# Sums of a chunk one step later, beside the other native products, and a new order of ScalarE's work in a graph layer

## The reference

```python
q = (x @ Wq).reshape(n, 8, 16)
wk = mlp2(edge_features, k_w1, k_b1, k_w2, k_b2)        # and wv: relu(e @ w1 + b1) @ w2 + b2
k = tensor_product(x[src], edge_sh, wk, Cqk)            # w * sum_{d,s} x[d] sh[s] C[d,s,:]; and v with wv, Cv
attn = einsum('ehd,ehd->eh', q[dst], k)
alpha = segment_softmax(attn, dst)
upd = segment_sum(v * alpha, dst) @ W_out
y = batchnorm(x @ W_self + upd) * gamma + beta
x1 = layernorm(x + y)
agg = segment_sum(e, dst) / max(count, 1)
out = layernorm(x1 + mlp3(concat([agg, x1])))
```

## Time and profile before

| | us |
|---|---|
| median of 3 runs (lowest, highest) | 5025.27 (5015.23, 5030.12) |
| the profiled execution's own time | 5049.76 |
| its span | 5047.8 |
| TensorE busy in the span | 4772.7 (95%) |
| VectorE, ScalarE, GpSimd busy | 4058.6, 3414.7, 3713.3 |

### The profile page before, as it was taken

One profiled execution on the slowest core, in us unless ns is written; L12 is line 12 of the kernel. 1 busy time (PEld: TensorE's weight loads), 2 busy tenths in 40 slices (PEclk: granted clock), 3 DMA queues, 4 the chain that ended last, 5 costly groups with the idle time before them and its releaser, 6 DMA issues. The chain is left out here.

```text
span 5047.8 us, 115383 instructions
## 1 busy us (share of the span) xinstructions
PE 4772.7 (95%) x35582; PEld 4503.5 (89%) x35582; DVE 4058.6 (80%) x5044; ACT 3414.7 (68%) x6495; POOL 3713.3 (74%) x3494
## 2 busy tenths in 40 slices
PE   7999999999999999999999999999999999998256
PEld 6999999999999999999999999999999999998143
DVE  5888888888888888888888888888888888886435
ACT  2677677677777767767777677777777777776137
POOL 3777777777777777777777777777777777774460
PEclk9999999999999999999999999999999999998578
DMA  8899999999999999999999999999999999996220
GB/s 218 202 215 210 208 210 214 208 214 210 212 207 214 213 208 213 211 210 211 211 213 211 207 216 213 216 214 214 213 216 212 214 214 216 212 213 158 91 68 26
DMA packets 693458, 1006.45 MB, mean 199 GB/s; under 512 B 120054, under 2 KB 378168, under 8 KB 693160
## 3 DMA queue, kind: packets, MB, share of 16 engines
q1 hardware_dynamic: 574856, 753.93, 65.7%
q0 software_dynamic: 112960, 242.16, 22.7%
q10 hardware_dynamic: 5600, 9.83, 0.7%
HBM read 826.64 MB, written 178.93 MB: 199 GB/s over the span
## 5 line engine op out<-in xcount | busy, mean ns | idle before, releaser
L825 PE MATMUL psum<-chi,zhi 128*128 128x256 f32 x7840 | 2316.9, 301 | 2.2 <-DVE rv L731 2.1
L535 POOL DMA_INDIRECT gq<-qtab,idxs x1568 | 1881.1, 1200 | 478.0 <-issue 475.8
L828 PE MATMUL psum<-clo,zhi 128*128 128x256 f32 x7840 | 2144.4, 282 | 0.0
L530 POOL DMA_INDIRECT gx<-in_xg,idxs x1568 | 1555.4, 992 | 465.0 <-issue 453.5
L827 PE MATMUL psum<-chi,zlo 128*128 128x256 f32 x6272 | 1768.4, 282 | 0.0
L825 PEld LDWEIGHTS psum<-chi,zhi 128*128 128x128 f32 x7840 | 1478.6, 189 | 99.3 <-issue 99.3
L828 PEld LDWEIGHTS psum<-clo,zhi 128*128 128x128 f32 x7840 | 1476.2, 188 | 0.0
L827 PEld LDWEIGHTS psum<-chi,zlo 128*128 128x128 f32 x6272 | 1183.6, 189 | 93.0 <-issue 93.0
L685 DVE TENSOR_TENSOR z<-psum,shb 128x1536 f32<-128x1536 f32 (+1 forms) x784 | 1130.5, 1483 | 126.2 <-PE psum L797 118.7
L580 ACT ACTIVATE zhi<-z 128x1536 fp32r<-128x1536 f32 (+1 forms) x784 | 993.5, 1267 | 247.9 <-DVE z L685 244.0
L710 DVE TENSOR_TENSOR zlo<-z,zhi 128x1536 fp32r<-128x1536 f32 (+1 forms) x784 | 922.2, 1217 | 0.0
(11 more groups left out here) (210 smaller groups left out, 6335.1 us busy)
## 6 DMA issues: line engine op xcount, KB each, us to landing
shb<-in_shT SPq DMA_DIRECT2D x392, 640.0 KB
shb<-in_shT SPq DMA_DIRECT2D x392, 512.0 KB
rows<-ot SPq DMA_DIRECT2D x392, 416.0 KB
e<-in_eT SPq DMA_DIRECT2D x392, 128.0 KB
drow<-rankd SPq DMA_DIRECT2D x392, 128.0 KB
gx<-in_xg,idxs POOLq DMA_INDIRECT x1568
gq<-qtab,idxs POOLq DMA_INDIRECT x1568
qtab<-qs ACTq DMA_DIRECT2D x25, 256.0 KB, 5.7
```

Source lines behind the costliest of these rows:

```text
L530: nc.gpsimd.indirect_dma_start(out=gx[:, s, k, :], out_offset=None, in_=xg[:, :], in_offset=bass.IndirectOffsetOnAxis(ap=ids[:, k:k + 1], ...
L535: nc.gpsimd.indirect_dma_start(out=gq[:, s, k, :], out_offset=None, in_=qtab[:, :], in_offset=bass.IndirectOffsetOnAxis(ap=ids[:, TC + k:T ...
L825: mm(tpb[:, k, :], zhi[:, s, j, e], chi[:, j, :], start=(j == 0), stop=False)
L828: last = mm(tpb[:, k, :], zhi[:, s, j, e], clo[:, j, :], start=False, stop=(j == ST - 1))
```

## The change

The sums of a chunk move to the next step (a = t - 7). On TensorE their first half goes to the head of the step and their second half behind `hidden(c)`, so that the native products stand together. On ScalarE the copies of the sums come first, `hid` and `hidhi` stand ahead of the second part of z, and `segments(b)` stands ahead of `feature_rows`. SyncE's store opens the step and is of chunk t - 8; `targets` is of chunk t - 5. The second mask tile `nmb` and its DMA go: the backward scan reads `nmf` shifted by one, with a last column set once to -1e30. The main stage has one more (mostly empty) step at its end.

```diff
@@ SyncE @@
-                        for ahead, tile in ((0, nmf), (1, nmb)):
-                            src = newd[bass.ds(g.value() * CH + ahead, GT * P)].rearrange("(t e) -> t e", t=GT)
-                            sp.dma_start(tile[:, s, :], src.unsqueeze(1).broadcast_to([GT, H, P])).then_inc(nm_in[s], 16)
+                        src = newd[bass.ds(g.value() * CH, GT * P)].rearrange("(t e) -> t e", t=GT)
+                        sp.dma_start(nmf[:, s, 0:P], src.unsqueeze(1).broadcast_to([GT, H, P])).then_inc(nm_in[s], 16)
...
                     def step(t, find, fetch, count):
+                        if (t + (-LAG - 2)).there():
+                            store(t + (-LAG - 2))
                         if (t + 2).there():
                             harmonics(t + 2)
                         if (t.r + 3) % 2 == 0 and (t + 3).there():
                             features(t + 3)
-                        if (t + (2 - LAG)).there():
-                            targets(t + (2 - LAG))
+                        if (t + (1 - LAG)).there():
+                            targets(t + (1 - LAG))
                         g = t + (-2)
                         if g.r % GC == 0 and g.there():
                             masks(g)
-                        if (t + (-LAG - 1)).there():
-                            store(t + (-LAG - 1))
@@ ScalarE @@
-                        c, b = t + 1, t + (-LAG)
+                        c, b, a = t + 1, t + (-LAG), t + (-LAG - 1)
+                        if a.there():
+                            sums(a, 0)
+                        if t.there():
+                            edge_weights(t)
                         if b.there():
                             weights(b)
-                        if t.there():
-                            edge_weights(t)
+                        if c.there():
+                            hidden(c)
+                        if a.there():
+                            sums(a, 1)
+                            maxima(a)
                         if c.there():
                             z_first_part(c, 0)
-                            hidden(c)
+                            hidden_first_part(c)
                             z_first_part(c, 1)
-                            hidden_first_part(c)
-                            if c.r % 2 == 1:
-                                feature_rows(c + (-1))
                         if b.there():
-                            sums(b, 0)
-                            maxima(b)
-                        if (b + 1).there():
-                            segments(b + 1)
-                        if b.there():
-                            sums(b, 1)
+                            segments(b)
+                        if c.there() and c.r % 2 == 1:
+                            feature_rows(c + (-1))
@@ VectorE @@
-                        v.tensor_tensor_scan(mr[:, ::-1], nmb[:, s, ::-1], mf[:, ::-1], -BIG, ALU.add, ALU.max).then_inc(mr_done, 1)
+                        v.tensor_tensor_scan(mr[:, ::-1], nmf[:, s, P:0:-1], mf[:, ::-1], -BIG, ALU.add, ALU.max).then_inc(mr_done, 1)
@@ TensorE @@
-                        c, b = t + 1, t + (-LAG)
+                        c, a = t + 1, t + (-LAG - 1)
+                        if a.there():
+                            sums(a, 0)
                         if c.there():
                             turned_x(c)
                             hidden(c)
+                        if a.there():
+                            sums(a, 1)
                         if t.there():
                             tensor_products(t)
                         if c.there() and c.r % 2 == 1:
                             turned_features(c + (-1))
-                        if b.there():
-                            sums(b, 0)
                         if c.there():
                             edge_weights(c)
-                        if b.there():
-                            sums(b, 1)
```

More of the change, by code:

```diff
@@ L92, in steps @@
             step(Chunk(i, R0 + k), *(m if k % GC == at else None for at in (0, 1, 3)))
-    for n in range(R0 + UN * TURNS, NC + LAG + 2):
+    for n in range(R0 + UN * TURNS, NC + LAG + 3):
         m = n - R0 - UN * TURNS + FINDS * TURNS
         step(Chunk(0, n), *(m if m <= NT else None,) * 2, m - 1 if FINDS * TURNS <= m - 1 <= NT else None)
-assert FINDS * TURNS + (NC + LAG + 1 - R0 - UN * TURNS) >= NT + 1 >= FINDS * TURNS
+assert FINDS * TURNS + (NC + LAG + 2 - R0 - UN * TURNS) >= NT + 1 >= FINDS * TURNS
 def gnn_kernel(nc, xg, xT, idx, dnow, dbefore, dlast, shT, eT, Wq, Ctp, W1, b1, Wk2, Wv2, b2, Wout, Wself, gamma_beta,
@@ L104, in gnn_kernel @@
     qtab = dram("qtab", (NP, O), fp32)
-    newd = dram("newd", (EP + P,), bf16)
+    newd = dram("newd", (EP,), bf16)
     chaind = dram("chaind", (EC,), fp32)
@@ L151, in gnn_kernel, with eb @@
         banks = [psum[:, i * 512:(i + 1) * 512] for i in range(8)]
+        edges = ctx.enter_context(ExitStack())
+        def eb(name, shape, dt=fp32):
+            return edges.enter_context(nc.sbuf_tensor(name, shape, dt))
+        chi = eb("chi", [P, ST, KV], f32r)
+        clo = eb("clo", [P, ST, KV], f32r)
+        w1 = eb("w1", [P, 2, P])
+        b1c = eb("b1c", [P, 1])
+        w2hi = eb("w2hi", [P, KV], f32r)
+        w2lo = eb("w2lo", [P, KV], f32r)
+        b2hl = eb("b2hl", [P, KV], f32r)
+        ones = eb("ones", [P, P], f32r)
+        idx_all = eb("idx_all", [P, 2 * EC], i32)
+        ndcol = eb("ndcol", [P, EC])
         load = sem("load")
@@ L229, in _ @@
                     sp.wait_ge(load, 16 * len(consts))
-                    sp.wait_ge(tables_stored, 64)
+                    sp.wait_ge(tables_stored, 48)
                 @block.tensor
@@ L306, in _ @@
                     v.memset(epsc[:, :], EPS)
-                    v.memset(npad[:, :], -BIG).then_inc(neg_made, 1)
                     dve.wait_ge(padded_made, 1)
@@ L783, in _ @@
                     v.memset(shb[D:P, :, ST - 1, :], 0.0).then_inc(shb_zero, 1)
-                    dve.wait_ge(shb_zero, 1)
+                    v.memset(nmf[:, :, P:P + 1], -BIG).then_inc(shb_zero, 1)
+                    dve.wait_ge(shb_zero, 2)
                     steps(dve, step)
@@ L885, in _ @@
                     steps(pe, step)
+        edges.close()
         with ExitStack() as mend:
@@ L1085, in gnn_kernel @@
             st_d, st_a, st_pe = sem("stats_dve"), sem("stats_act"), sem("stats_pe")
-            SS = {k: sem(f"{k}_made") for k in ("r", "y", "dd", "sq", "lg", "rs", "x1", "s0", "h0", "h1", "y2", "dd2", "sq2",
-                                                "lg2", "rs2", "o")}
-            prod_made = sem("products_made")
-            PRODUCTS = ("mean", "var", "z0", "z1", "z2", "mean2", "var2")
+            MADE = {"pe": ("mean", "var", "z0", "z1", "z2", "mean2", "var2"),
+                    "act": ("r", "sq", "lg", "rs", "h0", "h1", "sq2", "lg2", "rs2"),
+                    "dve": ("y", "dd", "x1", "s0", "y2", "dd2", "o")}
+            made_by = {e: sem(f"blocks_made_by_{e}") for e in MADE}
             def wait_made(engine, name, i, j):
-                if name in PRODUCTS:
-                    engine.wait_ge(prod_made, (i * len(PRODUCTS) + PRODUCTS.index(name)) * GN + (j + 1))
-                else:
-                    engine.wait_ge(SS[name], i * GN + (j + 1))
+                for e, names in MADE.items():
+                    if name in names:
+                        engine.wait_ge(made_by[e], (i * len(names) + names.index(name)) * GN + (j + 1))
             with ExitStack() as fin1:
@@ L1293, in product @@
                                 wait_made(pe, after, i, j)
-                                t.matmul(bank_of(j), lhsT[:, :], W(src, j), start=True, stop=True).then_inc(prod_made, 1)
+                                t.matmul(bank_of(j), lhsT[:, :], W(src, j), start=True, stop=True).then_inc(made_by["pe"], 1)
                         def turn(i):
```

39 lines of the change are left out of this document (13 added, 26 removed).

## The result

The changed kernel takes 4954.68 us (median of 4 runs, 4953.95 to 4955.17) against 5023.35 us before (4 runs, 5015.23 to 5030.12) on the same chip: 0.9863 of the time, 95% interval 0.984 to 0.9885. The profiled execution took 4955.06 us, 94.7 less than the one before, whose 5049.76 us lie above all four runs of that kernel.

A forecast was written before the change was run, and what follows sets the result against it. TensorE's queue was taken to bound the kernel at 11.53 us a step, with late gathers on top in most of the first 3000 us. All terms 0 except 10 us from gathers: 5025 - 10 = 5015 us, range 5003 to 5045.

The forecast's parts named there:

- the cost of the tensor products: TensorE's step: products start 0.120 us apart; none is added or removed, so the beat stays 11.53 us.
- The order on TensorE: Native products standing together: a change of kind costs 0.00 us, so 0, with a bound of 4 us of gain.
- rival 4: TensorE's order: fewer alternations save time that the starts don't show, 4 us or more, under 5010; chance 0.05.
- The late gathers: GpSimd's gathers for TensorE's transposes: of the 13.0 us above the floor about 10 go.
- My count of the delays: Gathers held by VectorE's two-operand ops in a step: 0.34 + 1.10 + 0.09 = 1.53 us after the change.
- one gather lost: Rival 2: VectorE's unbroken run of ops catches one gather more; 5038 to 5069 us; chance 0.15.
- Rival 2: GpSimd: one gather lost, 5038 to 5069 us; 0.1 us of error in `hidlo`'s start decides; chance 0.15.
- Second half of the sums: TensorE's wait for ScalarE's copy of the first half: cover 0.59 us, so 0; each 0.1 us beyond costs 39 us.
- SyncE and the masks: One of two mask DMAs goes and the store is a chunk later: 0.
- The ends: First stage 0, last stage 0, drain steps 0 with one step, 5.6 us, either way.
- The signs I named: `hidlo` under 0.4 us after `query_weights`, beat 11.53, gather waits under 10 us, no `ot` wait; beat under 11.5: order costs.

The follow-up runs named there:

- run 4: Kernel before with only ScalarE's order changed: hidden layer ahead of z's first part, its high part ahead of z's second; 5014.68 us (0.9967).
- run 8: run 4 with two 32-byte gaps, ahead of and behind the parts of z, which move these alone by 32 bytes; 4974.56 us (0.99).
- run 7: Changed kernel with two 32-byte gaps around the second layer's tables (behind `b1c` and behind `ones`); 5018.25 us.
- run 9: Changed kernel with the parts of z alone moved by 64 bytes; 5015.2 us.
- run 10: Changed kernel with the coefficient tables `chi` and `clo` moved by 64 bytes and all behind them by 128; 5016.26 us.
- run 2: Changed kernel with the second half of the sums ahead of the hidden layer's product on TensorE; 5146.7 us in one run.
- run 3: Changed kernel with all engines' orders put back, leaving the storage part, the mask's single DMA and small edits of first and last stage; 5071.68 us (1.0092).
- run 5: Kernel before with two 32-byte gaps, ahead of and behind the parts of z, which move these alone by 32 bytes; 5076.24 us (1.0104).
- run 1: Kernel before with the hidden layer's product ahead of the turns of x on TensorE; 5014.59 us (0.9986).
- run 17: Changed kernel with 128 bytes ahead of the parts of z and 128 behind, so that these alone move; 5023.46 us (1.0001).
- run 16: Changed kernel with the distance of 320 bytes modulo 512 between operands given to all float32r products; 5004.83 us (0.9951).
- run 11: Changed kernel with the parts of z and all behind them moved by 128 bytes; 4910.85 us in one run.
- run 18: run 4 with gaps of 160 bytes ahead of the parts of z and 96 behind, distance 320 modulo 512; 4934.81 us (0.9827).
- run 15: Changed kernel with a gap of 256 bytes ahead of the parts of z; 4950.75 us.

## Why the prediction was wrong

**The step that failed** is the cost of the tensor products. I read 0.120 us for one off and carried it over, and I gave no term at all to the parts of the diff that move operands: the region for the tables and the removed mask tile. Together they take the distance from 160 to 192 modulo 256. By the sizes the region moves it by 6656 bytes, which is 26 x 256 and changes nothing, and the mask by 480, so it is the tile `nmb`, which I had priced at 0 as a DMA, that shifts the weights; no run takes the mask alone. Where the gathers keep up, the shift is worth 40.1 us (run 4 to run 8, one edit of 64 bytes of gaps), 39 of them in the beat: 48 x (92.25 - 91.44). I had taken it that the beat stays since no product is added or removed, and that is false.

**The order on TensorE**, "0, bound 4 us". At the slow pace it held, as far as the runs reach: at 119.8 to 120.0 ns the new order gives 92.16 to 92.23 us (runs 7, 9, 10, at distance 0), the old 92.25 (distance 160); both orders at one such distance were not run. At 192 it does not hold: 91.44 becomes 90.83, 48 x 0.61 = 29 us. Of the 0.61, two steps in eight that run at 113.3 instead of 117.8 ns make 2 x 54 x 4.5 ns = 0.49. So the gain was neither an alternation saved (rival 4, to which I gave 0.05) nor visible in the old trace: it is a second pace that exists only at some distances, and that a step falls into or not by what stands ahead of it. That the order has a part in it is shown by run 2, where one edit of TensorE's order, which also brings a wait, takes the faster pace away. Of the 29 us the medians show 19.9 (run 8 to after): the changed kernel also waits 4.8 us for gathers in its first steps, and its last part, from the start of chunk 384 on, takes 509.4 us of span against 506.5 in run 8. The comparison of run 8 with after also holds the rest of the change (SyncE, the other moves on ScalarE, storage); between runs 3 and 5, which differ in the storage and the small edits, the beat moved by 0.1.

**The late gathers** were sized rightly: about 10 us forecast, 7 to 9 measured (run 4). That VectorE's wait for `hidhi`, which the new order closes, is what makes them late is not shown. For it speaks that ScalarE's order takes that wait from 510.7 to 82.9 us between runs 5 and 8, and the mean gather of the two tables from 1052 and 1143 ns to 1021 and 1055. Against it: in run 1 the wait stays and no gather is late, and in run 17 the wait is gone and 64.0 us of late gathers are there. What does go with them in every run is GpSimd's own sum. An estimate from the means of 500 to 4300 us: 66 gathers in eight steps, each with its 0.30 us of issue, need 66 x (1.098 + 0.30) = 92.3 us in run 5, 91.0 in run 17 and 90.8 in run 16, each more than its beat, and 92.2 before, just its beat. They need 89.9 in run 1, 88.3 in run 8, 88.9 after, 89.2 in run 11 and 87.4 in run 18, each less than its beat. By the rows of a step, a gather is longer where it meets one of VectorE's two-operand instructions. By the Trainium skill (SBUF — State Buffer, section "SBUF: two separate sides") a GpSimd instruction that reads SBUF is blocked while a VectorE instruction with two SBUF inputs that started before it runs. The trace after agrees: the gather of 3436.32 ends at 3437.64, 0.82 us after line 696 (3436.14 + 0.68 = 3436.82), though line 703 follows that line without a gap. My count of the delays had one gather caught by nearly the whole first `zlo`, 1.10 us. In the step shown a gather starts at 3437.95, 0.01 us ahead of that `zlo`, and takes its 0.94 us; the next meets only the end of `zlo` and loses 0.42. Hence 0.87 us of delay in that step and not 1.53, and the rival "one gather lost" did not come in the changed kernel. A gap of 0.01 us decided it. Rival 2 had named that doubt, and that it was decided well in this step was luck.

**What I had not foreseen about them** is their size once TensorE is faster. Alone, the new distance makes the kernel 1% slower (runs 3 and 5), since GpSimd then falls behind; alone, ScalarE's order gives 0.3% (run 4); together they take off 1.0% (run 8). Neither half has a worth of its own.

**Second half of the sums**: right, no wait in the trace. Run 2 shows its price without cover: a beat of 94.83 us instead of 90.83, 192 us in all, of which the lost faster pace explains 0.49 in eight steps. **SyncE and the masks**: nothing found. **The ends**: 0 plus or minus 5.6; a drain step grew by 0.92 us, 6.4 us in seven, a little past my bound. **The signs I named**: `hidlo`, the waits of line 802 under 10 us and no wait for `ot` came as written; the beat fell under 11.5, which I would have read as the cost of the order. More than half of the fall, 0.81 of 1.42 us, was something else.

**Still open.** Why the distance counts modulo 256 bytes, and what lets a step fall into the faster pace: only that both are so is shown. Why the mean gather was 1051 ns in run 11's one run and 1079 in run 17, with the same distance and almost the same beat: their tensors behind the parts of z differ by 128 bytes of place, and other steps run at 117.8 ns. So 4910.85 us is a single run and no version to rely on; 4934.81 is.

## What to carry to other kernels

Where TensorE sets the beat with float32r products, measure their start-to-start time in the trace and try a few gaps of 32 to 256 bytes ahead of the weights' tile: here that alone moved the beat from 92.25 to 90.60 us (runs 4 and 18), and a diff that moves or resizes a buffer can change the time by that alone. Before a bound is shortened, look for the engine that keeps up with it only just; here that was GpSimd, and a beat 0.9% shorter made the kernel 1% slower until a new order on ScalarE shortened the gathers. Test the halves of a change in all combinations: one by one they told of +1% and -0.3%, together of -1%.

## What the runs showed of the hardware

The interval of 128 x 128 by 256-column float32r products, weights and moving operand both from SBUF, depends on the distance of the two operands modulo 256 bytes (worked out from the tensors' sizes): 119.8 to 120.0 ns at 0 and 160, 118.5 to 120.0 at 128, 117.3 to 118.7 at 96, 116.8 at 224, 117.8 or 113.3 to 113.7 at 192 and 64, at the full granted clock. It is not the address (runs 10 and 11), and 256 bytes more change nothing (run 15). At 192 and 64 two paces exist, and a step keeps its own through all 54 intervals and, where no gather is late, in every turn. The edge weights, in groups of four, showed none of it: 117.6 to 118.5 ns after, 117.7 in run 16, where their distance was changed.

Behind many of TensorE's stops for late gathers (3.83 us in the one shown of run 5) the granted clock stood at 0.50, which is 1.2 GHz, so a stop cost more than its wait.
